# A causal mask for the chunks of maxima: triangles as weights and a 64x64 unit matrix moving, in place of the unit matrix as weights and the triangle moving

## What is computed

```python
x = x + attn_a0(norm(x))   # 16 heads of 64, one shared key/value head, no mask
x = x + ffn0(norm(x))      # input and weight rounded to FP6 in blocks of 32, one product
x = x + attn_b0(norm(x))   # 16 heads of 64, causal
x = x + ffn0(norm(x))
x = x + attn_a1(norm(x))   # 16 heads of 64, keys and values from a latent of 32, causal
x = x + moe(norm(x))       # 8 experts, top 2, and a shared one
x = x + attn_b1(norm(x))   # 16 heads of 64, biases, causal
x = x + moe(norm(x))

# a causal attention, per head:
logits  = q @ k.T / 8
logits  = where(key > query, -large, logits)
weights = softmax(logits)
out     = weights @ v
```

## Time and profile before

| | us |
|---|---|
| median of 3 executions | 2981.41 (2980.59 to 2983.26) |
| the profiled execution | 2981.51 |
| its span, first to last instruction | 2979.5 |
| TensorE (PE) busy | 2708.0 (91%) |
| VectorE (DVE) busy | 1835.3 (62%) |
| GpSimd (POOL) busy | 1490.1 (50%) |
| ScalarE (ACT) busy | 1181.8 (40%) |

### The profile page before, as it was taken

One profiled execution on the slowest core, in us unless ns is written; L12 is line 12 of the kernel. 1 busy time (PEld: TensorE's weight loads), 2 busy tenths in 40 slices (PEclk: granted clock), 3 DMA queues, 4 the chain that ended last, 5 costly groups with the idle time before them and its releaser, 6 DMA issues. The chain is left out here.

```text
span 2979.5 us, 41067 instructions
## 1 busy us (share of the span) xinstructions
PE 2708.0 (91%) x16065; PEld 1255.3 (42%) x16065; DVE 1835.3 (62%) x2337; ACT 1181.8 (40%) x1607; POOL 1490.1 (50%) x932
## 2 busy tenths in 40 slices
PE   4899999999948999999948999999687999999968
PEld 3333333333324444444424444444333444444433
DVE  2577677777573666666573677677543566666653
ACT  2444444444413444444412444444222444444422
POOL 1577777777703555555602556556201555555520
PEclk8899999999957999999957999999895999999979
DMA  4000000000000000000000000000000000000000
GB/s 104 1 1 1 1 1 1 1 1 1 0 16 1 1 1 1 1 1 1 1 15 14 1 1 1 1 1 1 1 0 1 1 1 1 1 1 1 1 1 14
DMA packets 21345, 14.63 MB, mean 5 GB/s; under 512 B 3233, under 2 KB 20001, under 8 KB 21026
## 3 DMA queue, kind: packets, MB, share of 16 engines
q1 hardware_dynamic: 21154, 12.01, 1.6%
HBM read 9.91 MB, written 2.10 MB: 4 GB/s over the span
## 5 line engine op out<-in xcount | busy, mean ns | idle before, releaser
L777 POOL TENSOR_TENSOR sums<-sums,p 128x1024 f32<-128x1024 f32 (+3 forms) x704 | 1367.9, 1943 | 730.5 <-PE ps L550 652.2
L692 DVE TENSOR_REDUCE half_max<-ps 128x2 f32<-128x1024 f32 (+3 forms) x640 | 696.9, 1089 | 547.0 <-PE ps L531 499.8
L507 PE MATMUL ps<-q,k 64*128 64x512 f32 (+3 forms) x3328 | 754.9, 532 | 0.0
L616 ACT ACTIVATE p<-ps 128x1024 f32<-128x1024 f32 (+3 forms) x704 | 585.3, 849 | 365.3 <-PE ps L510 198.9
L510 PE MATMUL ps<-max_row,pick 64*128 64x512 f32 (+3 forms) x1664 | 571.8, 684 | 0.0
L550 PE MATMUL ps<-p,v 128*64 128x512 f32 (+3 forms) x2816 | 565.8, 515 | 0.0
L712 DVE RECIPROCAL inverse<-total 128x128 f32<-128x128 f32 x512 | 477.7, 939 | 59.3 <-ACT total L657 48.9
L531 PE MATMUL ps<-k_near,q_near 64*128 64x512 f32 (+2 forms) x1664 | 369.6, 441 | 64.5 <-DVE half_max L692 47.9
L692 DVE TENSOR_REDUCE neg_max<-ps 128x2 f32<-128x256 f32 x192 | 158.6, 826 | 314.4 <-PE ps L536 314.4
L531 PEld LDWEIGHTS ps<-k_near,q_near 64*128 64x128 f32 x1664 | 160.9, 190 | 432.6 <-issue 281.4
L507 PEld LDWEIGHTS ps<-q,k 64*128 64x128 f32 x3328 | 293.3, 187 | 91.2 <-issue 66.3
(11 more groups left out here) (138 smaller groups left out, 2054.1 us busy)
## 6 DMA issues: line engine op xcount, KB each, us to landing
q_w<-in_wq SPq DMA_DIRECT2D x3, 512.0 KB
o_w<-in_wo SPq DMA_DIRECT2D x3, 512.0 KB
k_w<-in_wk SPq DMA_DIRECT2D x2, 512.0 KB
v_w<-in_wv SPq DMA_DIRECT2D x2, 512.0 KB
out<-x SPq DMA_DIRECT2D x4, 256.0 KB, 2.8
scratch<-in_wq_t SPq DMA_DIRECT2D x1, 512.0 KB, 5.3
scratch<-in_w_out SPq DMA_DIRECT2D x1, 512.0 KB, 7.6
wq_latent<-scratch SPq DMA_DIRECT2D x1, 512.0 KB, 3.3
```

Of the source, the lines that this page charges most:

```text
L507: nc.tensor.matmul(out[:, head, 0:width], a.k[rows, key_slot(i, 3), k * P:(k + 1) * P], a.q[rows, i % 3, s * BANK + lo:(s + 1) * BANK], st ...
L616: act.activation(probabilities(g)[:, :, lo:BANK], score[g % 2][:, :, 0:BANK - lo], ACT.Exp)\
L692: last = v.tensor_reduce(out, chunk_ps[:, :, 0:hi - lo], AX.X, ALU.max, negate=True)
L777: pool.tensor_tensor(sums, sums, probabilities(g)[:, :, lo:BANK], ALU.add).then_inc(summed, 1)
```

## The change

The four mask matmuls of a diagonal chunk take a triangle as weights (a new constant `a.later`, 128 partitions by 2 halves by 128 columns in bf16, with -1e30 where the key is later than the query) and the 64x64 unit matrix as moving operand. Each half writes its own 64 columns. The constant is made by GpSimd at the start of the first attention phase, `a0`: one fill and two selections, before GpSimd's other work of that phase. The new tensor lies between `neg_max` and `half_max` in SBUF.

```diff
-def attention_phase(nc, m, a, tag, dram, after, causal, biased=False, shared=False):
+def attention_phase(nc, m, a, tag, dram, after, causal, biased=False, shared=False, make_constants=False):
...
                 if diagonal:
                     for half in range(2):
                         for head, rows in enumerate(HEADS):
-                            last = nc.tensor.matmul(chunk_ps[:, head, hi - lo - P:hi - lo],
-                                                    a.shifted_ident[rows, half, :], a.causal[rows, half, :],
-                                                    start=False, stop=half == 1)
+                            at = hi - lo - P + half * HD
+                            last = nc.tensor.matmul(chunk_ps[:, head, at:at + HD], a.later[rows, half, :],
+                                                    a.shifted_ident[rows, 0, 0:HD], start=False, stop=half == 1)
                 last.then_inc(chunked, 1)
...
         @block.gpsimd
         def _(pool):
+            if make_constants:
+                blank, shaped = sem("blank"), sem("shaped")
+                pool.memset(a.later[:], 0.0).then_inc(blank, 1)
+                pool.wait_ge(blank, 1)
+                for rows in HEADS:
+                    pool.affine_select(out=a.later[rows], in_=a.later[rows], compare_op=ALU.is_ge, fill=MASKED,
+                                       base=0, pattern=[[-HD, 2], [1, P]], channel_multiplier=-1).then_inc(shaped, 1)
+                pool.wait_ge(shaped, 2)
...
+        a.later = sb("later", [P, 2, P], BF16)
...
-        attention("a0", causal=False, shared=True)
+        attention("a0", causal=False, shared=True, make_constants=True)
```

## The result

The changed kernel takes 2961.65 us (median of 4, 2956.47 to 2963.94) against 2981.59 before (median of 4, 2980.59 to 2983.26): a ratio of 0.993, 95% interval 0.9913 to 0.9947. Two further comparisons gave 2962.84 (0.9936, 0.9924 to 0.9949) and 2963.47 (0.9932, 0.9920 to 0.9945). So it is some 19 to 20 us faster, where 2960.4 was forecast. The profiled execution has a span of 2957.5 us, 22.0 less than before's, and its own time was 2959.47.

The account below looks back on a forecast made before the run. TensorE was taken to bound the kernel, busy 91% of the span; 18.6 us from full-clock groups plus 2.4 from half-clock heads made 21.0 us saved, nothing added, so 2960.4 us, range 2957 to 2966.

Parts of the forecast that it names:

- TensorE bounds the causal bodies, one wait per item: In causal bodies TensorE sets the time, waiting only at chunk 9 of each item, 0.43 us, for chunk 8's maximum.
- 0.054 us per group, from start to start: Each full-clock group of four mask matmuls saves 0.054 us (0.05 to 0.06); 344 kept groups give 18.6 us.
- A group lost in each item of a2 to VectorE's chain, 0.9 us: In a2 VectorE reaches chunk 8 late, so chunk 7's mask saving is swallowed: one group of eight, 16 in all.
- forecast of 0.38 per item in a2: The a2 item period falls by 7 x 0.054 = 0.38 us, with one of eight groups lost.
- The heads at half clock, 0.108 per group: At the causal phases' heads, 22 groups at 1.2 GHz save twice the price: 22 x 0.108 = 2.4 us.
- The prelude and the shift in SBUF, 0: GpSimd's fill and two selections in a0, and 512 bytes per partition of SBUF shift, cost 0; without cover the prelude costs 1.3.
- The sum: Whole kernel: 18.6 + 2.4 = 21.0 us saved, giving 2960.4 us; 83% chance as worked out.
- the upper end: Largest saving for the whole kernel, at 0.06 us per group: 23.4 us, that is 2958.0 us.
- A: VectorE takes back half of the groups' saving in the items: 10.6 us saved, 2970.8 us; 7%.
- B: Fewer columns don't shorten the mask group, because weights or issue set its pace: nothing saved, 2981.4 us; 3%.
- C: TensorE's clock falls to half once within a body, one item taking some 36 us more: +15 net, 2996 us; 3%.
- the Trainium skill's floor of about 25 ns from start to start: Contrary rule for the mask matmuls: four would take 0.10 us, so the edit would save 8 us, 2973.

Follow-up runs that it names:

- odd-only kernel: Changed kernel with the new mask form only on odd-numbered diagonal chunks, the old form on even ones; one execution 2967.1 us, beside 2983.73 for the kernel before.
- The third profile: Changed kernel run a third time without edit, beside the variant with the constant made in the setup phase; median 2963.47 us.
- after_again: Changed kernel run a second time, no edit; median 2962.84 us of 5.

## Why the prediction was right, and which steps were off

- **TensorE bounds the causal bodies, one wait per item.** Right. The body is full at a clock of 1.00, and the periods of the changed kernel repeat to 0.03 us in its three profiles.
- **0.054 us per group, from start to start.** Right for six groups of eight: 425 to 369 ns at chunk 1. The score mask of line 515 was the right row to read. Mis-sized for the two ahead of scores, 594 to 564 at chunk 0 and 916 to 888 at chunk 2: there 0.028 of the 0.056 to 0.058 come back in the product behind, and 0.028 to 0.030 are left. The step that failed was to stop at the start of the next group. Read one group further, to line 510, it shows in the profile after; before, nothing showed a short mask behind which the product wasn't delayed already. The loads' rows could have warned: the product's load starts with the last pair, and the last pair moves by one pair's columns only, not by two. 96 groups less 6 in the heads, times 0.025, are 2.3 us that the sum had too much.
- **A group lost in each item of a2 to VectorE's chain, 0.9 us.** Wrong. The row of the maximum of chunk 8 at 1823.45 bore no note of a wait, and was read as held up by the work ahead of it. But the maximum hung on the chunk. The kernel before, then the changed one, in a2:

```profile
1822.52 0.94 DVE L712 RECIPROCAL inverse<-total 128x128 f32<-128x128 f32 x1
1822.91 0.50 PE L531 MATMUL ps<-k_near,q_near 64*128 64x512 f32 x2
1823.45 1.23 DVE L692 TENSOR_REDUCE half_max<-ps 128x2 f32<-128x1024 f32 x1
...
1809.83 0.94 DVE L712 RECIPROCAL inverse<-total 128x128 f32<-128x128 f32 x1
1810.16 0.51 PE L531 MATMUL ps<-k_near,q_near 64*128 64x512 f32 x2
1810.71 1.23 DVE L692 TENSOR_REDUCE half_max<-ps 128x2 f32<-128x1024 f32 x1
```

The maximum starts 0.54 us behind the chunk (1822.91 to 1823.45), as in a1, where VectorE had been idle. Where VectorE itself sets the pace, its next row starts 0.08 us before the end of the one ahead (in the last item of each phase, 82 to 84 ns); here it was 0.01 before and 0.06 to 0.08 after. So VectorE had some 0.07 us to spare, and the change used nearly all of it. In the odd-only kernel a2's item fell by 0.33, six groups' worth. The forecast of 0.38 per item in a2 was met at 0.39 by luck: one group too few was counted, and two were counted at twice their worth. Only in the last item of each phase is chunk 7's group lost, as forecast, though the wait that swallows it is chunk 8's, not chunk 9's: chunk 8 there starts 1336 ns behind the last pair of matmuls ahead of it (line 550) before and 1405 after, in a1.
- **The heads at half clock, 0.108 per group.** Right: from the first mask to the second chunk 1.04 us before (896.33 to 897.37) and 0.93 after:

```profile
898.24 0.33 PE L537 MATMUL ps<-shifted_ident,later 64*128 64x64 bf16 x4
899.17 0.58 PE L531 MATMUL ps<-k_near,q_near 64*128 64x256 f32 x2 [0.61 <-DVE neg_max L692]
```

- **The prelude and the shift in SBUF, 0.** Right in its effect, as far as the runs can tell: 1.0005 (0.9996 to 1.0014). GpSimd's first rounding came at 47.08, not at about 45.6, but behind a wait of 0.74 us for ScalarE's copy of the slow projection. The selections took 0.83 us in place of 0.45, and ended more than 20 us ahead of the first chunk.
- **The sum.** With what the runs showed it is (272 - 3) full-clock groups x 0.054 + 90 x 0.029 + 22 x 0.108 = 14.5 + 2.6 + 2.4 = 19.5 us, beside 19.8 and 19.9 measured from first to last chunk. The forecast's 21.0 was 1.5 too high by two errors that went against each other, 2.3 too much ahead of scores and 15 x 0.054 = 0.8 too little in a2. The third profile gives 19.4. By phase the agreement is worse: the runs' terms come to 6.5 us in each, and the first profile has 6.0, 7.7 and 6.1. In a2 the half clock lasted 26.2 us from the first chunk on before and 22.5 after, and 22.4 to 24.1 in all kernels with a shorter mask or none; whether the shorter mask brings this or chance does isn't shown. So the total's 0.3 us is in part luck. The further 2.2 us of the first profile's span lie outside the causal stretches, where they come and go with the profile (after_again has 1.6 us more there than the kernel before), and the median of the runs fell by 19.9. A small slip: with 0.06 per group the upper end is 23.3, not 23.4.
- **The rivals.** A: no wait grew outside the last items; even without any mask, 0.70 us less per item, the interval at chunk 9 stayed at 0.49 to 0.50. B: fewer columns did shorten the group in full. But weights, those of the product behind, seem to set the pace ahead of scores, so B's mechanism holds in part for 90 groups. By the Trainium skill's floor of about 25 ns from start to start ("TensorE: Matmul & The Clock Gate", section "Wait — 56ns, not 53.3ns?") the group of four would have held an estimated 0.10 us; it held 0.06 to 0.07 (1142.33 to 1142.39), so the trace disagrees with it here too. The two heads' matmuls start 3 to 6 ns apart and the pairs 29 to 39, so the trace doesn't speak against such a floor for each half of the rows. C: the clock was 1.00 in the bodies.

A hint for a further version lies in the kernel without a chunk mask, at 2923.64 us. Softmax doesn't depend on which number is subtracted, as long as the exponentials of a row's real keys don't all vanish; a maximum that takes in up to 127 later keys is such a number, if the scores' spread is bounded. Whether it is depends on the inputs, and that was not studied here.

## What to carry to other kernels

Price a short matmul from its start to the start of the next, and then one group further: what follows may pay for it. Here a mask of half the columns gave its whole 54 ns ahead of one kind of product and half of it ahead of another. Look at the loads of weights as well: in the changed kernel the group ended 58 ns earlier, but the load behind it started only some 32 ns earlier. And a row without a note of a wait doesn't say that its engine was late; compare the moment in which its input was ready, and how far its row overlaps the one ahead, before a chain is built on it.

## What the runs showed of the hardware

- The time of a product (line 507) depends on the matmul just ahead of it. At chunk 0 (256 columns) it is 300 ns to the next group behind a last pair of 128 columns and 327 behind 64, whatever stood ahead of that pair; at chunk 2 (512 columns) it is 513 and 541, and 455 behind the unmasked chunk of 384 columns.
- The first load of a product's weights started within 2 ns of the last pair of masks ahead of it, and line 510 came 353 to 355 ns behind that load at chunk 0 in four kernels (one of them without a mask), 365 and 368 in the two with a single pair.
- Having a mask group at all costs some 17 ns beyond its columns ahead of a full-row product (295 without, 340 with one pair of 64, and of these 45 the next pair of 64 takes only 29).
- With the same kernel the thin stretch between a1 and a2 took 117.0 and 121.3 us in two profiles, at granted clocks of 0.66 and 0.62, and over all kernels the first projection of a0, unchanged in each, took 1.10 or 2.05 us. The dense bodies, at 1.00, agreed to 0.03 us per item. This scatter sets how well a fraction of a per cent can be measured here: the items' periods tell 0.05 us apart where medians of five executions fail at 4 us.
